# Extra identity products around the typed counts of a max pass over lanes, in a four-layer graph network

## The chip, the cores and the metric

The kernel runs on one core of one Trainium2 chip. Its time is the device time of one execution in microseconds; before the change it is 4076.91 us, the median of three runs (4075.01, 4076.91 and 4076.97 us).

## The reference

Four graph layers follow each other on 6,250 nodes of 128 values and 106,250 edges that are sorted by destination, with a residual and a layer normalisation after each. The change touches the third layer, whose core is a maximum over the edges of each node:

```python
msgs = z[edge_dst] @ Wd + z[edge_src] @ Ws + edge_weight[:, None] * ww[None, :] + bm
agg = jax.ops.segment_max(msgs, edge_dst, num_segments=n)
agg = jnp.where(deg[:, None] > 0, agg, 0)
hidden = jax.nn.relu(z @ W1[:H] + agg @ W1[H:] + b1)
x = layernorm(x + hidden @ W2 + b2)
```

The fourth layer sums messages whose weights depend on the type of an edge (0 or 1). For it the kernel builds matrices of counts, how many edges of a type go from a node to a node; these are the typed counts, and they are built during the max pass, for 27 of the 49 tiles of 128 nodes.

## The kernel before

**The max pass.** The edges are dealt out to 128 lanes (partitions), so that a lane holds a run of successive edges. Column `i` of all lanes is one step, and there are 831 steps, worked through in 208 chunks of four. A chunk passes through these engines:

- GpSimd (POOL) issues for each step one indirect DMA (L1834) that gathers the 128 source rows of the step, 512 bytes each, into `LANE_ROWS`, a ring of 32 steps. The instruction waits until the gather 16 steps back has landed, and at the first step of a chunk until TensorE is done with the chunk eight chunks back (semaphore `l2_turned`). GpSimd also gathers the maxima of finished nodes (L1822), and at the end of each of six segments a row per lane (L1806), for which it waits until the stored history of the last chunks of the segment has landed.
- TensorE (PE) puts the messages of a chunk into one of banks 0 to 2, in `messages`: a bf16 product for the edge weights (L1628, 512 columns) and one of the f32 identity with the gathered rows (L1631, 512 columns, which the trace shows as two matmuls), whose end raises `l2_turned`. It does this one chunk ahead of the rest.
- VectorE (DVE) takes the running maximum of the four steps out of the bank (L1711, four instructions that follow each other) into a history, which SyncE (SP) stores to memory. It raises `l2_scanned`.
- TensorE then makes one unit of typed counts, in `tensor_typed_counts`: eight bf16 products of one-hot matrices (L1153, 64 rows, 98 columns each), into banks 5 and 7. The last raises `typed_counted`. A unit waits until ScalarE has emptied the banks of the unit before (`typed_units`) and, for every other unit, for one-hot matrices that VectorE makes (L1168).
- ScalarE (ACT) empties the two banks with two casts (L1212) as soon as `typed_counted` is up, and raises `typed_units`.

So TensorE's order in the loop is: messages of chunk c+1, typed counts of chunk c, then the node work that a hand-made schedule (`max_schedule`) puts behind chunk c: transposes (L550), products with the f32 weights (L575, L1606, L1607). A chunk that ends a segment has a product more (`carry`, L1639), into columns 0 to 127 of bank 3 (`CARRY`), which ScalarE copies out (semaphore `rotations`). Columns 128 to 511 of bank 3 are not used in the pass.

The other layers multiply dense matrices of counts with rows split in three bf16 pieces; L2106 and L2125 are their products, of 384 columns in most layers, and L2171 their gathers on GpSimd.

Of the kernel before, what the change touches and what calls it, by code (L numbers as in the profile page):

```python
# [14 lines left out]
P = 128  # L15
# [28 lines left out]
CH = 4  # L44
# [83 lines left out]
SEGMENT = [0] + [-(-(-(-START[g] * N_ET // NT) + SEGMENT_MARGIN) // CH) * CH for g in SEGMENT_GROUPS[:-1]] + [N_ET]  # L128
SEGMENTS = len(SEGMENT_GROUPS)
# [4 lines left out]

FIRST_BANKS = ((0, 1), (2, 3))
CARRY = 3

# [78 lines left out]
def low(g):  # L218
    return banks_of(g)[:len(banks_of(g)) // 2]


def high(g):
    return banks_of(g)[len(banks_of(g)) // 2:]


def region(buf, g, width, half=0):
    words = GMAX * H2 // (2 if g >= NG - 2 else 1)
    at0 = (words if g == NG - 1 else 0) + half * words // 2
    return buf[:, at0:at0 + GROUPS[g] * width]


def blocks(buf, g, q, k=1):
    return [region(buf, g, k * P)[:, (k * q + b) * P:(k * q + b + 1) * P] for b in range(k)]
# [6 lines left out]
def parts(g, per):  # L240
    return [(b, q, min(per, GROUPS[g] - q)) for b, q in enumerate(range(0, GROUPS[g], per))]
# [135 lines left out]
def chunk_tiles(c):  # L377
    return range(c * CH, min((c + 1) * CH, N_ET))
# [166 lines left out]
def turn(k, g, src, width, banks, sem):  # L545

    n = 0
    for j in gtiles(g):
        for b in range(width // P):
            t = k.nc.tensor.transpose(k.bank[banks[n // 4]][:, n % 4 * P:(n % 4 + 1) * P],  # L550
                                      src(j)[:, b * P:(b + 1) * P], k.IDENT)
            n += 1
    t.then_inc(sem, 1)
# [16 lines left out]
def products(k, g, left, right, width, banks, sem):  # L570

    per = 512 // width
    for q in range(GROUPS[g]):
        for i, block in enumerate(left(q)):
            t = k.nc.tensor.matmul(k.bank[banks[q // per]][:, q % per * width:(q % per + 1) * width], block, right[i],  # L575
                                   start=i == 0, stop=i == len(right) - 1)
    t.then_inc(sem, 1)
# [546 lines left out]
def message_banks(g):  # L1124

    return (banks_of(g)[0], banks_of(g)[2]) if len(banks_of(g)) == 4 else banks_of(g)


def typed_unit(c):

    return divmod(c + UNITS, UNITS) if 0 <= c < UNITS * (len(TYPED) - 1) else None
# [6 lines left out]
def typed_banks(i, u):  # L1138
    return FIRST_BANKS[u % 2] if i == 0 else TYPED_BANKS


def tensor_typed_counts(k, i, u):

    T, unit, quarter = k.nc.tensor, UNITS * i + u, 4 * i + u // 2
    if u % 2 == 0:
        T.wait_ge(k.sem("typed_onehot"), quarter + 1)
    if i or u >= 2:
        T.wait_ge(k.sem("typed_units"), unit if i else unit - 1)
    for n in range(4):
        c = (4 * u + n) % QUARTER  # L1150
        for h in range(2):
            at = slice(REC * h, REC * h + REC)
            t = T.matmul(k.bank[typed_banks(i, u)[h]][:, n * KEYS:(n + 1) * KEYS], k.TSRC[quarter % 2][at, c, :],  # L1153
                         k.TKEY[quarter % 2][at, c, :], start=True, stop=True)
    t.then_inc(k.sem("typed_counted"), 1)
# [417 lines left out]
def parts_loaded(k, n):  # L1573
    return k.sem(f"load_parts_{n % 2}"), 16 * (n // 2 + 1)
# [20 lines left out]
def max_tensor(k, p):  # L1595
    T = k.nc.tensor

    def node(stage, g):
        if stage == "turn":
            T.wait_ge(*p.at("present", g))  # L1600
            turn(k, g, k.acc(H), H, low(g), p.sem(stage))
        elif stage == "first":
            T.wait_ge(*p.at("copy", g))
            for b, q, n in parts(g, 4):
                o = k.bank[high(g)[b]][:, 0:n * P]
                T.matmul(o, k.w1_2[:, 0, :], k.AUX3[:, START[g] + q:START[g] + q + n, :], start=True, stop=False)  # L1606
                t = T.matmul(o, k.w1_2[:, 1, :], region(k.ZT, g, P)[:, q * P:(q + n) * P], start=False, stop=True)  # L1607
            t.then_inc(p.sem(stage), 1)
        elif stage == "second":
            T.wait_ge(*p.at("relu", g))  # L1610
            products(k, g, lambda q: blocks(k.HT, g, q), [k.w2_2[:]], H, low(g), p.sem(stage))
        elif stage == "xturn":
            T.wait_ge(*p.at("normalise", g))
            turn(k, g, k.xt, H, high(g), p.sem(stage))
        elif stage == "parts":
            T.wait_ge(*p.at("xcopy", g))
            products(k, g, lambda q: [k.aux(START[g] + q)], [k.wdc[:, :, :].rearrange("p k h -> p (k h)")], H2,
                     message_banks(g), p.sem(stage))

    def messages(c):  # L1620

        tiles = chunk_tiles(c)
        n, slot, batch = len(tiles), tiles[0] % MAX_RING, c // PART_CHUNKS
        bank = k.bank[c % MAX_BANKS][:, 0:n * P]
        if c >= MAX_BANKS:
            T.wait_ge(k.sem("l2_scanned"), CH * (c - MAX_BANKS + 1))
        T.wait_ge(*parts_loaded(k, batch))
        T.matmul(bank, k.W9[:, batch % 2, c % PART_CHUNKS, :], k.WW9[:, 0:n * P], start=True, stop=False)  # L1628
        for i in tiles:
            T.wait_ge(*p.landed(i))  # L1630
        T.matmul(bank, k.IDENT, k.LANE_ROWS[:, slot:slot + n, :].rearrange("p t c -> p (t c)"), start=False,  # L1631
                 stop=True).then_inc(k.sem("l2_turned"), 1)

    def carry(s):

        T.wait_ge(k.sem("l2_scanned"), SEGMENT[s + 1])
        if s:
            T.wait_ge(k.sem("rotations"), 1 + s)
        T.matmul(k.bank[CARRY][:, 0:P], k.ROTATE, k.HIST[:, (SEGMENT[s + 1] - 1) % MAX_RING, :], start=True,  # L1639
                 stop=True).then_inc(k.sem("l2_carried"), 1)  # L1640

    T.wait_ge(k.sem("rotations"), 1)
    messages(0)
    for c in range(NCH):
        if c + 1 < NCH:
            messages(c + 1)
        if chunk_tiles(c)[-1] + 1 in SEGMENT:
            carry(SEGMENT.index(chunk_tiles(c)[-1] + 1) - 1)
        tensor_typed_counts(k, *typed_unit(c))
        for stage, g in p.due.get(c, ()):  # L1650
            node(stage, g)
    T.wait_ge(k.sem("typed_units"), UNITS * len(TYPED))
    for stage, g in p.tail:
        node(stage, g)
# [92 lines left out]
def max_scalar(k, p):  # L1747
# [29 lines left out]
    def carry(s):  # L1777

        A.wait_ge(k.sem("l2_carried"), s + 1)
        if s:  # L1780
            A.wait_ge(k.sem("l2_fixed"), s)
        A.copy(k.CARRIED, k.bank[CARRY][:, 0:P]).then_inc(k.sem("rotations"), 1)

# [1402 lines left out]
def dense_sync_l3(k, p):  # L3186
# [33 lines left out]
    "l1a": (dense_tensor_l1a, dense_vector_l1a, dense_scalar_l1a, dense_gpsimd_l1a, dense_sync_l1a),  # L3220
    "l1b": (dense_tensor_l1b, dense_vector_l1b, dense_scalar_l1b, dense_gpsimd_l1b, dense_sync_l1b),
    "l2": (max_tensor, max_vector, max_scalar, max_gpsimd, max_sync),
    "l3": (dense_tensor_l3, dense_vector_l3, dense_scalar_l3, dense_gpsimd_l3, dense_sync_l3),
}
# [694 lines left out]
```

## Time and profile before

| | |
|---|---|
| median of three runs | 4076.91 us |
| the profiled execution | 4070.89 us |
| its span, first to last instruction | 4066.8 us |
| TensorE, recorded busy | 2772.3 us, 68% |
| GpSimd, recorded busy | 2381.6 us, 59% |
| mean granted TensorE clock | 0.807 |
| the max pass in the span | about 1985 to 3400 us |

The profile is of one execution. "Idle before" is the time in which an engine did nothing recorded ahead of an instruction, and "<-" names what ended it: an instruction of another engine whose end lies just before, "issue" where no wait shows, and "remote" (in the chain "another core or an unknown queue") where the semaphore rose but no instruction that raises it had just ended. With one core there is no other core. The granted clock is a share of 2.4 GHz and has two levels, 1.00 (2.4 GHz) and 0.50 (1.2 GHz). Ends of matmuls are worked out by the profiler from their size; ends on the other engines are observed.

### The profile page before, as it was taken

The numbers are of one execution on the slowest core, as the hardware profiler recorded it, in microseconds if no ns is written. First come the engines' busy times: TensorE is split into PE (matmuls) and PEld (weight loads), VectorE is DVE, ScalarE is ACT, GpSimd is POOL, SyncE is SP. The second block draws the span as 40 slices with busy tenths as digits, with TensorE's granted clock in tenths as the row PEclk, the third lists the DMA queues.
The fourth block names the chain that finished last, engine by engine and source line by source line (L and its number), as shares of the span: only waits on it lengthen the run. The fifth ranks groups of instructions, "written<-read, shape, count | busy, mean of one in ns | idle before, by whom it ended". The sixth has DMA issues, their size and how long they took to land.

```text
span 4066.8 us, 48309 instructions
## 1 busy us (share of the span) xinstructions
PE 2772.3 (68%) x18224; PEld 1669.8 (41%) x18224; DVE 1410.9 (35%) x3599; ACT 854.8 (21%) x2326; POOL 2381.6 (59%) x2389
## 2 busy tenths in 40 slices
PE   3788787888798888888344443453453435989897
PEld 2444444555566777777111111121121112545454
DVE  6555564223231122212233332342343323233332
ACT  2555553222230111101111111221121112000000
POOL 3665662656626666664466656656555561777775
PEclk6899999889899999999555555665666556999998
DMA  5454444655546666664533432343343326656563
GB/s 149 152 175 153 162 168 157 194 179 187 189 154 206 202 196 195 201 201 141 145 125 125 143 124 86 124 133 116 111 129 125 113 93 222 227 198 230 198 224 128
DMA packets 299413, 658.89 MB, mean 162 GB/s; under 512 B 76555, under 2 KB 181976, under 8 KB 291624
## 3 DMA queue, kind: packets, MB, share of 16 engines
q1 hardware_dynamic: 188808, 404.50, 28.6%
q0 software_dynamic: 106784, 248.47, 21.3%
q8 instruction: 150, 2.46, 0.3%
q10 hardware_dynamic: 3584, 2.75, 0.2%
q14 instruction: 87, 0.71, 0.1%
HBM read 456.83 MB, written 198.69 MB: 161 GB/s over the span
## 4 chain that ended last, share of the span: by engine, by line
PE 47%; another core or an unknown queue 25%; issue 13%; ACT 8%; DVE 6%; DMA 1%; POOL 0%; ACTq 0%; SPq 0%; POOLq 0%; DVEq 0%
PE banks L2106 27%; PE banks L575 4%; PE banks L2127 4%; PE banks L2125 3%; PE banks L1631 3%; ACT arena L1212 3%; PE banks L550 1%; PE banks L2220 1%; ACT arena L2415 1%; PE banks L1153 1%; ACT x_nodes L612 1%; PE banks L1628 1%; ACT junk L624 1%; DVE arena L1711 1%
## 5 line engine op out<-in xcount | busy, mean ns | idle before, releaser
L2106 PE MATMUL banks<-arena 128*128 128x384 bf16 (+1 forms) x9310 | 1533.4, 313 | 119.5 <-issue 108.6
L2106 PEld LDWEIGHTS banks<-arena 128*128 128x128 bf16 x9310 | 906.6, 100 | 594.8 <-issue 203.4
L1834 POOL DMA_INDIRECT arena<-tab_l,ring_of_rows x831 | 798.7, 961 | 421.0 <-issue 281.1
L2171 POOL DMA_INDIRECT arena<-h_pieces,span_sources x450 | 434.6, 966 | 320.8 <-issue 111.4
L2171 POOL DMA_INDIRECT ring_of_rows<-message_pieces,span_sources x396 | 426.2, 1076 | 206.2 <-issue 100.1
L1153 PE MATMUL banks<-arena 64*128 64x98 bf16 x1728 | 98.5, 251 | 553.1 <-ACT arena L1212 349.5
L1711 DVE SCALAR_TENSOR_TENSOR arena<-arena,ring_of_rows,banks 128x128 f32<-128x128 f32 x830 | 288.2, 347 | 528.5 <-remote 233.3
L2171 POOL DMA_INDIRECT ring_of_rows<-x_pieces,span_sources x306 | 331.6, 1084 | 202.1 <-PE banks L2125 99.0
L2171 POOL DMA_INDIRECT ring_of_rows<-l_pieces,span_sources x306 | 298.1, 974 | 237.2 <-issue 70.9
L1212 ACT CAST arena<-banks 128x392 bf16<-128x392 f32 x432 | 188.3, 489 | 1157.3 <-remote 780.4
L1631 PE MATMUL banks<-arena,consts 128*128 128x512 f32 x416 | 361.0, 964 | 95.1 <-DMA arena<-tab_l,ring_of_rows 77.8
L2151 DVE TENSOR_TENSOR arena<-iota_bf,span_targets 128x768 bf16<-128x768 bf16 x243 | 134.9, 556 | 807.3 <-remote 343.7
L1153 PEld LDWEIGHTS banks<-arena 64*128 64x128 bf16 x1728 | 58.2, 114 | 810.1 <-issue 563.7
L2125 PE MATMUL banks<-ring_of_rows,arena 128*128 128x384 bf16 x1008 | 268.0, 335 | 16.9 <-issue 12.2
L2415 ACT CAST arena<-banks 128x392 bf16<-128x392 f32 x512 | 217.2, 493 | 197.9 <-PE banks L2220 117.0
L2127 PE MATMUL banks<-arena 128*128 128x256 bf16 x1350 | 182.1, 277 | 13.2 <-issue 12.9
L559 ACT COPY zt<-banks 128x512 f32<-128x512 f32 (+2 forms) x108 | 56.5, 549 | 588.9 <-remote 310.9
L1631 PEld LDWEIGHTS banks<-arena,consts 128*128 128x128 f32 x416 | 91.0, 272 | 179.1 <-issue 179.1
L550 PE MATMUL banks<-consts,arena 128*128 128x128 f32 x343 | 60.0, 311 | 130.5 <-DVE arena L659 50.4
L2127 PEld LDWEIGHTS banks<-arena 128*128 128x128 bf16 x1350 | 133.5, 99 | 36.3 <-issue 18.4
L1168 DVE TENSOR_TENSOR arena<-second_iota_bf,arena 128x784 bf16<-128x784 bf16 x108 | 60.7, 562 | 251.1 <-remote 228.9
L624 ACT ACTIVATE junk<-arena 128x256 bf16<-128x256 f32 (+1 forms) x196 | 73.9, 378 | 349.4 <-DVE arena L2859 138.7
(260 smaller groups left out, 2620.2 us busy)
## 6 DMA issues: line engine op xcount, KB each, us to landing
arena<-edge_counts SPq DMA_DIRECT2D x83, 896.0 KB
arena<-edge_counts SPq DMA_DIRECT2D x83, 672.0 KB
running_max<-arena SPq DMA_DIRECT2D x207, 256.0 KB
edge_counts<-arena SPq DMA_DIRECT2D x32, 1568.0 KB
typed_counts<-arena SPq DMA_DIRECT2D x27, 1568.0 KB
arena<-typed_counts SPq DMA_DIRECT2D x27, 896.0 KB
arena<-typed_counts SPq DMA_DIRECT2D x27, 672.0 KB
arena<-tab_l,ring_of_rows POOLq DMA_INDIRECT x831
```

Of the source, the lines that this page charges most:

```text
L575: t = k.nc.tensor.matmul(k.bank[banks[q // per]][:, q % per * width:(q % per + 1) * width], block, right[i], start=i == 0, stop=i == len(r ...
L1153: t = T.matmul(k.bank[typed_banks(i, u)[h]][:, n * KEYS:(n + 1) * KEYS], k.TSRC[quarter % 2][at, c, :], k.TKEY[quarter % 2][at, c, :], sta ...
L1212: t = A.copy(nodes[:, :, :, h, :], k.bank[typed_banks(i, u)[h]][:, 0:4 * KEYS].rearrange("p (i s r) -> p s i r", i=4, r=2))
L1631: T.matmul(bank, k.IDENT, k.LANE_ROWS[:, slot:slot + n, :].rearrange("p t c -> p (t c)"), start=False, stop=True).then_inc(k.sem("l2_turne ...
L1711: V.scalar_tensor_tensor(k.HIST[:, i % MAX_RING, :], before, k.SAME[:, i:i + 1], message, ALU.min, ALU.max).then_inc(k.sem("l2_scanned"), 1)
L1834: G.indirect_dma_start(k.LANE_ROWS[:, i % MAX_RING, :], None, k.tab["l2"], bass.IndirectOffsetOnAxis(ap=k.LANE_SRC[:, i:i + 1], axis=0)).t ...
L2106: t = T.matmul(k.bank[i % N_SUMS][:, 0:rows.shape[-1]], counts[:, s, :], rows, start=s == 0 and n == 0, stop=s == NT - 1 and n == len(term ...
L2125: return T.matmul(bank[:, 0:3 * H], weights, three, start=first, stop=last)
L2127: done = T.matmul(bank[:, 0:H2], weights, three[:, n * H2:(n + 1) * H2], start=first and n == 0, stop=last and n == 2)
L2151: V.tensor_tensor(k.OHG[p.layer][:, b % 2 * BATCH:(b % 2 + 1) * BATCH, :].rearrange("p c (v d) -> p c v d", d=2), k.IOTAB.rearrange("p (v ...
L2171: G.indirect_dma_start(k.rows[p.layer][s % n], None, k.pieces[p.layer], bass.IndirectOffsetOnAxis(ap=k.SRCG[:, at:at + 1], axis=0)).then_i ...
L2415: t = A.copy(nodes[:, :, :, h, :], k.bank[banks[h]][:, 0:4 * KEYS].rearrange("p (i s r) -> p s i r", i=4, r=2))
```

## The change

In the max pass TensorE gets two bf16 products ahead of the typed counts of a chunk and two behind them, each of the bf16 identity with the identity read three times: 128 rows, 128x128 weights, 384 columns. They write columns 128 to 511 of bank 3, which nothing reads, and raise no semaphore. Around the end of each segment two chunks are left out, so that the products keep clear of the copy of `carry`; with the constants of this kernel these are chunks 69, 70, 119, 120, 153, 154, 170, 171, 187, 188, 206 and 207, which leaves 196 chunks of 208. Ahead of the products of the chunks after a segment's end stands a wait for that copy.

```diff
+KEPT = 2
...
+    def keep_busy(n, c):
+
+        carried = [s for s in range(SEGMENTS) if c >= chunk_tiles(SEGMENT[s + 1] // CH - 1)[0] // CH]
+        if carried and c < SEGMENT[carried[-1] + 1] // CH + 1:
+            return
+        if carried:
+            T.wait_ge(k.sem("rotations"), 1 + len(carried))
+        for _ in range(n):
+            T.matmul(k.bank[CARRY][:, P:4 * P], k.IDB, k.IDB.unsqueeze(1).to_broadcast([P, 3, P]), start=True, stop=True)
+
...
         if chunk_tiles(c)[-1] + 1 in SEGMENT:
             carry(SEGMENT.index(chunk_tiles(c)[-1] + 1) - 1)
+        keep_busy(KEPT, c)
         tensor_typed_counts(k, *typed_unit(c))
+        keep_busy(KEPT, c)
         for stage, g in p.due.get(c, ()):
             node(stage, g)
```

## Rows read from the trace of the kernel before

**Rows 1.** The page: the span, and the granted clock in forty slices.

```profile
span 4066.8 us, 48309 instructions
...
PEclk6899999889899999999555555665666556999998
```

**Rows 2.** Busy time by stretch: the whole pass, then four short stretches.

```profile
core 0: us, PE busy (x) PEld busy (x) DVE busy (x) ACT busy (x) POOL busy (x), PEclk, DMA share, GB/s
1989.00:3390.00 1401.00, 615.57 (x2603) 222.66 (x2602) 492.54 (x1328) 240.25 (x549) 833.17 (x867) 0.60 0.37 119
2076.40:2081.40 5.00, 4.77 (x22) 1.75 (x22) 3.60 (x12) 1.84 (x5) 4.04 (x4) 0.50 0.31 93
2081.40:2085.20 3.80, 3.67 (x24) 1.09 (x22) 3.59 (x11) 0.87 (x2) 2.83 (x3) 1.00 0.50 153
2095.30:2104.60 9.30, 0.00 (x0) 0.00 (x0) 1.19 (x4) 0.00 (x0) 4.72 (x5) 0.50 0.25 71
2126.40:2137.90 11.50, 11.43 (x44) 3.34 (x40) 8.30 (x24) 2.62 (x6) 6.92 (x8) 0.50 0.35 115
```

**Rows 3.** Groups of instructions, forms kept apart, 1985 to 3400 us.

```profile
line engine op names shapes xcount | busy us, mean ns | idle before us <-releasers
L1834 POOL DMA_INDIRECT arena<-tab_l,ring_of_rows x816 | 784.2, 961 | 397.6 <-issue 257.7 <-remote 95.0 <-PE banks L1631 44.9
...
L1212 ACT CAST arena<-banks 128x392 bf16<-128x392 f32 x416 | 181.7, 489 | 1152.4 <-remote 780.4 <-issue 199.2 <-PE banks L1153 172.7
...
L1606 PE MATMUL banks<-arena 128*128 128x512 f32 x22 | 22.8, 1141 | 71.3 <-ACT zt L559 69.9 <-issue 1.5
```

**Rows 4.** Who waited for whom, 1985 to 3400 us.

```profile
engine line waited for: us in total, times, longest us
ACT arena L1212 <- remote: 780.4, 67, 41.7
...
PE banks L1153 <- ACT arena L1212: 348.0, 44, 24.4
...
POOL arena L1806 <- DMA running_max<-arena: 125.5, 6, 27.5
...
POOL running_max L1812 <- DVE arena L1720: 38.2, 5, 8.8
```

**Rows 5.** Timeline, chunks whose counts are taken at once, clock 0.50.

```profile
start us, us, engine line op out<-in xcount [idle before <-releaser]
2105.61 0.51 PE L1153 MATMUL banks<-arena 64*128 64x98 bf16 x8 [10.38 <-ACT arena L1212]
...
2106.16 0.87 ACT L1212 CAST arena<-banks 128x392 bf16<-128x392 f32 x2 [0.61 <-PE banks L1153]
...
2108.48 0.51 PE L1153 MATMUL banks<-arena 64*128 64x98 bf16 x8
...
2111.35 0.51 PE L1153 MATMUL banks<-arena 64*128 64x98 bf16 x8
```

**Rows 6.** Timeline, two chunks at clock 1.00.

```profile
2081.89 0.35 PE L1153 MATMUL banks<-arena 64*128 64x98 bf16 x8
...
2083.44 0.35 PE L1153 MATMUL banks<-arena 64*128 64x98 bf16 x8
```

**Rows 7.** Timeline, a chunk whose counts are taken late.

```profile
2092.32 0.51 PE L1153 MATMUL banks<-arena 64*128 64x98 bf16 x8 [7.25 <-ACT arena L1212]
...
2093.16 2.07 PE L1631 MATMUL banks<-arena,consts 128*128 128x512 f32 x2
...
2100.48 0.94 POOL L1834 DMA_INDIRECT arena<-tab_l,ring_of_rows  x1 [0.30 <-issue]
2104.68 0.87 ACT L1212 CAST arena<-banks 128x392 bf16<-128x392 f32 x2 [12.51 <-remote]
...
2105.45 0.94 POOL L1834 DMA_INDIRECT arena<-tab_l,ring_of_rows  x1 [4.02 <-remote]
```

**Rows 8.** Timeline, typed counts when GpSimd has just begun to gather.

```profile
1967.31 0.87 ACT L1212 CAST arena<-banks 128x392 bf16<-128x392 f32 x2 [0.50 <-PE banks L1153]
```

**Rows 9.** The chain in order of time, fourth layer: start, us, what.

```profile
3567.68 4.07 PE banks L2106 x12
...
3600.08 2.27 PE banks L2106 x14
```

**Rows 10.** Who waited for whom in the fourth layer, 3450 us to the end.

```profile
ACT zt L559 <- remote: 181.0, 8, 41.5
```

## The prediction

> **What bounds the kernel now.** I read the page first, then the busy time by stretch, the groups and waits of the max pass, the timeline and the chain. The page [rows 1] shows one long stretch, the max pass, in which TensorE's clock is granted at 0.5 to 0.6; everywhere else it is near full. By stretch [rows 2] the pass takes 1401 us, mean grant 0.60, and TensorE is recorded busy for 616 us of it, GpSimd for 833. Nobody is saturated, so the reader should look for a loop of waits.
>
> GpSimd's own floor: a gather is 0.94 us and 0.30 us to the next [rows 7], 1.25 us with rounding, so four steps are 5.0 us a chunk. 831 gathers, 49 of maxima and 12 at segment ends make 892 x 1.25 = 1115 us. The other 300 us or so of the pass is GpSimd waiting: 398 us idle before L1834 less 816 x 0.30 = 153 us [rows 3], and 125.5 + 38.2 us at the ends of segments [rows 4]. These are waits for the chunks to get through TensorE, VectorE and the history store.
>
> TensorE's side: at clock 0.50 free-running chunks follow each other every 2.87 us (counts start at 2105.61, 2108.48, 2111.35) and ScalarE takes the counts within 0.04 us of their recorded end [rows 5]. At clock 1.00 a chunk is 1.55 us [rows 6]. Either is faster than the 5.0 us of gathers, so TensorE ought to keep up. It does not because of what rows 7 show: the counts of 2092.32 have a recorded end at 2092.83, but ScalarE gets its semaphore at 2104.68, twelve us later, after GpSimd too had stopped and waited 4.02 us. TensorE recorded nothing in between (fourth stretch of [rows 2]). I call this a held release. Over the pass ScalarE lost 780 us in 67 such waits of 208 [rows 4], and TensorE's next unit waited behind ScalarE. Where GpSimd has only just begun to gather, the counts are taken at once [rows 8]. In the timeline the held releases lie inside long runs of gathers and end when such a run has stopped for want of ring space (3.2 us after it in rows 7); then some three chunks run freely, GpSimd restarts with the first of them, and a few us later the next release is held. The same happens in the fourth layer while TensorE streams products [rows 10], so a busy TensorE does not prevent it. I don't know its mechanism; that it belongs to the gathers is a reading.
>
> The Trainium skill (Perfetto Trace Analysis, Tensor Engine Instruction) says that the end shown for a matmul is computed, and that the semaphore goes up only when PSUM has acknowledged the write. Rows 7 agree that the two can part, here by 12 us; the page gives no cause, and the sum goes by ScalarE's observed start.
>
> **The change part by part.** It removes and moves nothing. It adds 196 x 4 = 784 products of 384 columns. Price: in the fourth layer 14 products of that size take 2.27 us, 0.162 us each, at clock 1.00; with the clock partly at 0.50 12 take 4.07 us, 0.34 each [rows 9]. I take 0.16 and 0.32, thus 0.65 or 1.3 us a chunk, 127 or 255 us of TensorE in all. Weight loads overlap, as in those rows.
>
> (a) Chunks whose release is held. The two products behind a unit and the two ahead of the next go out before TensorE blocks on `typed_units`, so they fall into the hold. With holds of 12 us on average (780/67) their 1.3 us is covered: nothing. If the cover were gone they would cost 67 x 1.3 = 87 us at most.
>
> (b) Chunks that run freely. 208 less 67 is 141; part of the 36 waits "for issue" (199 us [rows 3]) are holds whose semaphore record is missing, so I take 120. There TensorE is the bound of the burst: each product lengthens it, and late next are `l2_turned`, hence VectorE's maximum, the history store and GpSimd's ring, and `typed_counted`, hence ScalarE. A chunk is 4.17 us at 0.50 and 2.20 us at 1.00 against 2.87 and 1.55 now. Now the free chunks average about 2.6 us (2.87 mostly, 1.55 in the few full-clock stretches).
>
> (c) The clock. It decides (b). TensorE was recorded busy 4.77 of 5.00 us at 0.50 and then got 1.00; elsewhere 11.43 of 11.50 us, and stayed at 0.50 [rows 2]. So bursts stand at the edge of being granted full speed, and 384-column streams in the narrow-product part of a chunk should tip more of them. But a burst starts after an idle hold, so its beginning is at 0.50 whatever follows, 5 us of it in the one case where the grant rose (second stretch of [rows 2]). I take 1.2 chunks at 4.17 and 1.4 at 2.20: mean 3.1 us, 0.5 us more than now. 120 x 0.5 = 60 us.
>
> (d) What GpSimd absorbs. The timeline shows runs of 16 to 24 gathers, 4.6 chunks on average, with a 4 us wait behind each [rows 7]; they give now 5.0 + 4/4.6 = 5.9 us a chunk without the segment ends. If a slower burst costs a run 0.8 chunk, it is 5.0 + 4/3.8 = 6.05, and 208 x 0.18 = 37 us. Between 60 and 37 I take the middle, as I have no row that separates them: 48 us.
>
> (e) f32 node products in the second half (L1606 at 1141 ns [rows 3]) gain if the clock is up: at most a few tens of us; I take nothing, since they follow the same idle time. The wait for `rotations` stands two chunks behind the copy that ends it: nothing; upper bound, the 6 copies' 1 us each.
>
> Sum: profiled execution 4070.9 + 48 = 4119 us (span 4066.8 + 48 = 4115). The median lies 6 us above the profiled execution, so on it 4077 + 48 = 4125; I give 4122.
>
> **Bounds.** Everything free stays at 0.50: 120 x 1.3 = 156 us, 4233. All free chunks at full clock: 120 x (2.20 - 2.6) = -48 us, and with some 30 us from the node products -80, 4000.
>
> **Rivals.**
> 1. *Full clock carries the pass (faster).* The products keep TensorE granted at 1.00 from early in each burst: -48 to -80 us, 3997 to 4029. It decides once more than about four fifths of the free chunks run at full speed (4.17 - 1.97 x 0.8 = 2.6). For it: the edge seen in (c). Against: holds of 5 to 15 us with nothing to do, which four products of 1.3 us cannot fill. The Trainium skill (TensorE: Matmul & The Clock Gate, The HAM clock gate) holds that the half rate is the default and sustained activity lifts it; by that this rival is what the change would do, up to the idle gaps, which it says bring the half rate back. The drop to 0.50 by 2095.3 after an idle stretch [rows 2] agrees with the second part. Chance 0.24.
> 2. *Work behind the counts shortens the holds (faster).* In the fourth layer eight of ScalarE's waits are held [rows 10], but TensorE never stops there. If more matmuls behind a unit bring its semaphore up sooner, say 2 us in each of 67 holds, 134 us go, 3943; the floor is 1115 us plus the segment ends' 164. Against: the 12 us of rows 7 passed with a f32 product behind the counts already. Chance 0.10.
> 3. *The clock does not move (slower).* 4190 to 4233. For it: 11.43 of 11.50 us at 0.50. Chance 0.16.
> 4. *No change that shows.* The bursts' loss is all covered by GpSimd's 5.0 us a chunk, which also a chunk of 4.17 us does not exceed. For it: that very comparison. Against: GpSimd waits 300 us for TensorE's side. Chance 0.14.
> 5. My forecast, 4090 to 4170: chance 0.36.
>
> **How the numbers follow.** The measurement tells about 0.2%, 8 us. Slower 0.36 + 0.16 = 0.52, within 0.2% 0.14, faster 0.34. The range leaves out the extremes of rivals 2 and 3: 3990 to 4205. The likeliest case's own range is 4090 to 4170.
>
> **What the profile after would show.** Right: 784 new matmuls of 384 columns; free chunks at about 4.2 us at 0.50 and 2.2 at 1.00; mean grant in the pass up from 0.60 to some 0.65 to 0.75; about 60 to 75 waits of ScalarE "remote" with 700 to 800 us; GpSimd's waits in the pass up by some 50 us; nothing changed before 1985 us or in the fourth layer. Wrong, if the grant goes above 0.8 (rival 1), if ScalarE's remote waits fall by over 100 us (rival 2), or if GpSimd's idle time is what it was (rival 4).

## The result and the profile after

The changed kernel takes 4117.59 us, median of four runs (4102.11 to 4120.86), beside 4075.96 us for the kernel before in the same session (four runs, 4067.33 to 4076.97): a ratio of 1.0099 with a 95% interval of 1.007 to 1.0129, some 42 us slower. The profiled execution is the fastest of the four, 4102.11 us, so its trace shows only 31 us of the 42.

The page of the changed kernel, which answers to [rows 1]: span, granted clock in forty slices, and the groups of the new products (line, engine, operation, names, shapes, count, then busy us, mean ns and idle time before).

```profile
span 4098.2 us, 49877 instructions
...
PEclk6899998899999999999676766676676666999999
...
L1643 PE MATMUL banks<-identity_bf 128*128 128x384 bf16 x784 | 247.3, 406 | 0.0
...
L1643 PEld LDWEIGHTS banks<-identity_bf 128*128 128x128 bf16 x784 | 70.7, 112 | 184.2 <-issue 162.2
```

All 784 products are there. The slices of the pass went from 5 and 6 tenths to 6 and 7. Outside the pass the clock line is as it was, but for a tenth here and there.

Busy time by stretch of the changed kernel: the pass, all before it, all behind it (columns as in [rows 2]).

```profile
1989.00:3421.00 1432.00, 749.31 (x3357) 277.68 (x3357) 490.81 (x1327) 237.68 (x542) 846.56 (x875) 0.68 0.36 117
0.00:1985.00 1985.00, 1601.34 (x12385) 1118.27 (x12385) 702.47 (x1858) 569.41 (x1666) 1104.64 (x1108) 0.91 0.55 176
3421.00:4098.00 677.00, 568.57 (x3273) 330.37 (x3266) 216.58 (x415) 47.63 (x119) 434.41 (x403) 0.93 0.60 207
```

TensorE is recorded busy for 749 us in the pass, 134 more than in [rows 2], and its mean grant is 0.68 after 0.60. To place the 31 us I take three marks of each trace: the first typed counts of the pass, round which the first new products stand, the end of the last gather, and the end. Before, they lie at 1989.0, 3363.5 and 4066.8 us; after, at 2000.7, 3398.6 and 4098.2. So 12 us of the difference were there before the first added product, in code that is the same; 23 us lie in the pass, and 4 us came back behind it. A single pair of traces can't say more: the four runs of this kernel lie up to 19 us apart, and those of the kernel before up to 10, later up to 38. The same mark lies at 1995.1 to 2002.1 us in the traces of e1 to e4 below and at 2013.2 in that of h1, so what lies ahead of the pass scatters by as much as the pass itself grew here.

Who waited for whom in the changed kernel, 1985 to 3421 us, against [rows 4].

```profile
ACT arena L1213 <- remote: 841.9, 76, 49.0
...
PE banks L1154 <- ACT arena L1213: 386.6, 44, 36.8
...
POOL arena L1847 <- remote: 104.8, 32, 8.8
...
POOL arena L1847 <- PE banks L1632: 60.4, 29, 10.1
```

The held releases are still there, 76 for 842 us after 67 for 780. They did not go away. These waits are ScalarE's idle time, which also holds the time until TensorE has made the counts; how late ScalarE is behind the recorded end of the counts is the last column of the table below.

TensorE's timeline in the changed kernel: two chunks at half clock, a restart after a held release, two at full clock, and the next restart.

```profile
2089.43 0.51 PE L1154 MATMUL banks<-arena 64*128 64x98 bf16 x8 [8.98 <-ACT arena L1213]
2089.87 0.82 PE L1643 MATMUL banks<-identity_bf 128*128 128x384 bf16 x2
2090.62 0.61 PE L1629 MATMUL banks<-arena 36*128 36x512 bf16 x1
2091.16 2.07 PE L1632 MATMUL banks<-arena,consts 128*128 128x512 f32 x2
2093.03 0.85 PE L1643 MATMUL banks<-identity_bf 128*128 128x384 bf16 x2
2093.81 0.51 PE L1154 MATMUL banks<-arena 64*128 64x98 bf16 x8
...
2113.09 0.51 PE L1154 MATMUL banks<-arena 64*128 64x98 bf16 x8 [8.27 <-ACT arena L1213]
...
2117.05 0.35 PE L1154 MATMUL banks<-arena 64*128 64x98 bf16 x8
2117.34 0.50 PE L1643 MATMUL banks<-identity_bf 128*128 128x384 bf16 x2
...
2119.47 0.35 PE L1154 MATMUL banks<-arena 64*128 64x98 bf16 x8
...
2127.47 0.51 PE L1154 MATMUL banks<-arena 64*128 64x98 bf16 x8 [5.51 <-issue]
```

And the same stretch on ScalarE and GpSimd.

```profile
2112.07 0.87 ACT L1213 CAST arena<-banks 128x392 bf16<-128x392 f32 x2 [9.79 <-remote]
```

```profile
2108.74 0.94 POOL L1847 DMA_INDIRECT arena<-tab_l,ring_of_rows  x1 [0.30 <-issue]
2112.85 1.20 POOL L1847 DMA_INDIRECT arena<-tab_l,ring_of_rows  x1 [3.17 <-remote]
```

A free chunk now takes 4.38 us at the half clock (2089.43 to 2093.81), where [rows 5] had 2.87, and 2.42 us at the full one (2117.05 to 2119.47), where [rows 6] had 1.55. The pattern is that of [rows 7]: release held, gathers stop (the last one shown ends at 2109.68), release 2.4 us later, burst. The bursts begin at the half clock again (0.51 us for the counts at 2113.09 and 2127.47, after 8.3 and 5.5 us without work). In the second burst shown the counts run at full clock from its second chunk, in the first not yet. Over the whole pass, each of the 47 pauses of TensorE of over 5 us in this trace, and each of the 48 in the trace before, is followed by work at the half clock.

### The profile page after: what moved, and what is told of

It is laid out like the page before. It is cut to its first block, busy times and chain, and to the rows that moved or that the text cites. A ratio compares the mean times of both kernels' runs of the same rounds, so it can differ in the third digit from the quotient of the medians.

```text
span 4098.2 us, 49877 instructions
## 1 busy us (share of the span) xinstructions
PE 2919.2 (71%) x19008; PEld 1726.3 (42%) x19008; DVE 1409.9 (34%) x3599; ACT 854.7 (21%) x2326; POOL 2388.7 (58%) x2389
## 4 chain that ended last, share of the span: by engine, by line
PE 48%; another core or an unknown queue 23%; issue 12%; ACT 7%; DVE 6%; POOL 1%; DMA 1%; SPq 1%; ACTq 0%; POOLq 0%; DVEq 0%
PE banks L2119 27%; PE banks L576 4%; PE banks L2138 3%; PE banks L2140 3%; PE banks L1632 3%; ACT arena L1213 2%; PE banks L551 1%; PE banks L1643 1%; PE banks L2233 1%; POOL arena L1847 1%; ACT arena L2428 1%; PE banks L1154 1%; ACT junk L625 1%; PE banks L1629 1%
## 5 line engine op out<-in xcount | busy, mean ns | idle before, releaser
L2119 PE MATMUL banks<-arena 128*128 128x384 bf16 (+1 forms) x9310 | 1553.7, 315 | 129.9 <-issue 117.2
L1632 PE MATMUL banks<-arena,consts 128*128 128x512 f32 x416 | 309.6, 834 | 80.8 <-DMA arena<-tab_l,ring_of_rows 67.8
L1643 PE MATMUL banks<-identity_bf 128*128 128x384 bf16 x784 | 247.3, 406 | 0.0
L1643 PEld LDWEIGHTS banks<-identity_bf 128*128 128x128 bf16 x784 | 70.7, 112 | 184.2 <-issue 162.2
```

What stands on the lines that cost most here:

```text
L1643: T.matmul(k.bank[CARRY][:, P:4 * P], k.IDB, k.IDB.unsqueeze(1).to_broadcast([P, 3, P]), start=True, stop=True)
L2119: t = T.matmul(k.bank[i % N_SUMS][:, 0:rows.shape[-1]], counts[:, s, :], rows, start=s == 0 and n == 0, stop=s == NT - 1 and n == len(term ...
```

## The experiments

The kernels ran in four groups, each on one chip (e1 to e4, f1 to f4, g1 to g3, h1: four different ones) with runs of the kernel before beside them. Ratios are against those. For what lies inside the pass I count from the trace of each profiled execution: the pass runs from the first chunk that can have new products to the end of the last gather; a chunk is free when ScalarE begins on its counts less than 0.6 us after their recorded end, otherwise held; its pitch is the time to the next chunk's counts; "ScalarE late" is the sum over the held ones of how late it began. Each row on the pass is one execution, and the row "before" is the trace of the first session, whose chip is not on record. The traces are not all alike in how fast their execution was: e2's and h1's traces are of the slowest of their runs (4106.33 and 4188.93 us beside medians of 4087.08 and 4172.89), the changed kernel's is of its fastest (4102.11 beside 4117.59).

| kernel | before beside it, us | ratio (95%) | pass, us | grant in the pass | free chunks | their pitch: mean, median us | ScalarE late, us |
|---|---|---|---|---|---|---|---|
| before | | | 1374 | 0.60 | 119 | 3.79, 2.87 | 764 |
| changed | 4075.96 | 1.0099 (1.007 to 1.0129) | 1398 | 0.68 | 115 | 4.23, 3.88 | 735 |
| e1, four and four | 4078.74 | 1.0107 (1.0081 to 1.0133) | 1414 | 0.76 | 108 | 4.41, 3.07 | 723 |
| e2, ahead only | 4078.74 | 1.0014 (0.9993 to 1.0034) | 1398 | 0.66 | 113 | 3.94, 3.38 | 764 |
| e3, behind only | 4078.74 | 1.0025 (1.0001 to 1.005) | 1382 | 0.64 | 121 | 3.85, 3.64 | 714 |
| e4, 16 columns | 4078.74 | 1.0061 (1.0041 to 1.0081) | 1402 | 0.56 | 108 | 4.14, 3.17 | 742 |
| h1, eight and eight | 4080.55 | 1.0228 (1.0201 to 1.0255) | 1456 | 0.83 | 114 | 4.98, 4.37 | 626 |
| f1, GpSimd 16 ahead | 3447.20 | 1.0 (0.9987 to 1.0013) | 1111 | 0.59 | 207 | 5.40, 5.05 | 0 |
| f2, GpSimd 24 ahead | 3447.20 | 1.0 (0.999 to 1.0009) | 1110 | 0.58 | 207 | 5.40, 5.06 | 0 |
| g1, the change again | 3449.30 | 0.9989 (0.9978 to 1.0) | 1107 | 0.76 | 206 | 5.35, 4.93 | 1 |
| g2, as f1 | 3449.30 | 0.9995 (0.9986 to 1.0004) | 1111 | 0.58 | 207 | 5.39, 5.05 | 0 |
| f3, direct transfers | 3447.20 | 0.8742 (0.8726 to 0.8758) | 666 | 0.82 | 188 | 3.12, 2.48 | 29 |
| f4, f3 with the change | 3447.20 | 0.8824 (0.881 to 0.8839) | 687 | 0.91 | 205 | 3.40, 2.42 | 2 |
| g3, as f3 | 3449.30 | 0.8764 (0.875 to 0.8779) | 668 | 0.81 | 189 | 3.15, 2.49 | 26 |

### Place and number: e1, e2, e3

In e1 the number of products on either side is doubled; in e2 the call behind the counts is left out, in e3 the one ahead.

```
e1:  -KEPT = 2
     +KEPT = 4
e2:       tensor_typed_counts(k, *typed_unit(c))
     -    keep_busy(KEPT, c)
e3:  -    keep_busy(KEPT, c)
          tensor_typed_counts(k, *typed_unit(c))
```

> KEPT = 4: four products ahead of the typed counts and four behind, 1568 in all, twice the change. Column theory (each product costs its columns in the chunks that run freely, at the clock that is granted then): a free chunk is 5.5 us at 0.50 and 2.85 us at 1.00, against 4.2 and 2.2 with the change and 2.87 and 1.55 before; with half of them at full clock the mean is 4.2 us, 1.6 us over the 2.6 of before, but GpSimd's 5.0 us a chunk hides part: +90 to +150 us against before (4165 to 4225). Clock rival: with so many columns the full clock is kept through whole bursts, a free chunk is 2.85 us, and the loss is not larger than that of the change: +0 to +45 us, mean grant in the pass over 0.80.

> Two products ahead of the typed counts, none behind: half of the change. Column theory: half of its cost, +15 to +30 us against before, wherever the two stand. Place rival 1 (the products ahead delay the counts and with them ScalarE, the ones behind delay only the next messages, which VectorE takes later anyway): this half carries all of the loss, +35 to +45 us. Place rival 2 (the messages' end, which frees GpSimd, is what counts): both halves stand before the next messages, so again half of the loss.

> Two products behind the typed counts, none ahead. Column theory: +15 to +30 us against before, the same as the two ahead. Place rival 1: about 0. Rival that work behind the counts brings their semaphore up sooner: faster than before, ScalarE's remote waits under 700 us.

Either half costs 0.14% or 0.25% (8 and 7 us by the medians, where 15 to 30 were expected) with overlapping intervals, of which e2's includes no change. So no place is favoured. The half behind the counts did not make the kernel faster, and ScalarE's waits in its trace stayed above the 700 us under which they would have spoken for an earlier release (who waited for whom in e3, 1985 to 3400 us):

```profile
ACT arena L1213 <- remote: 751.7, 65, 38.6
```

The whole costs 0.99%, more than the two halves together (0.39%), but it was measured in another session and in four runs. Doubling it costs 1.07% (42 us), no more than the change itself within the intervals: in time the clock rival came true and not the 90 to 150 us of the column theory, though the grant stayed under the 0.80 that the rival asked for. The clock line of e1 shows the rise:

```profile
PEclk6899998899999999999687776786777777999999
```

The pass has 7 and 8 tenths now, 0.76 on average. With more full-clock chunks the median pitch of e1's free chunks is 3.07 us, under the 3.88 us of the changed kernel, though it has four products more; its mean is 4.41 against 4.23.

### The products without their columns: e4

The same 784 products with 16 columns in place of 384: the instructions and the weight loads stay, the streaming nearly goes.

```
-            T.matmul(k.bank[CARRY][:, P:4 * P], k.IDB, k.IDB.unsqueeze(1).to_broadcast([P, 3, P]), start=True, stop=True)
+            T.matmul(k.bank[CARRY][:, P:P + 16], k.IDB, k.IDB[:, 0:16], start=True, stop=True)
```

> The change with its 784 products cut from 384 columns to 16: same instructions, weight loads and wait, hardly any columns. Column theory: a free chunk is some 0.1 to 0.25 us longer (four weight loads of 0.1 us, in part overlapped), thus 0 to +15 us against before, and the mean grant in the pass stays at 0.60. Instruction rival (the number of instructions or weight loads, or the wait for the copy, is what costs): +30 to +45 us like the change.

It already costs 0.61%, some 26 us, where 0 to 15 were expected for next to no columns and 30 to 45 if the instructions were the whole cost: it lies between the two. Its timeline on TensorE at the half clock:

```profile
2106.20 0.51 PE L1154 MATMUL banks<-arena 64*128 64x98 bf16 x8 [3.81 <-ACT arena L1213]
2106.64 0.22 PE L1643 MATMUL banks<-identity_bf 128*128 128x16 bf16 x2
2106.80 0.60 PE L1629 MATMUL banks<-arena 36*128 36x512 bf16 x1
2107.33 2.07 PE L1632 MATMUL banks<-arena,consts 128*128 128x512 f32 x2
2109.20 0.25 PE L1643 MATMUL banks<-identity_bf 128*128 128x16 bf16 x2
2109.38 0.51 PE L1154 MATMUL banks<-arena 64*128 64x98 bf16 x8
...
2112.55 0.51 PE L1154 MATMUL banks<-arena 64*128 64x98 bf16 x8
```

A chunk takes 3.17 us against 2.87 in [rows 5]: 0.30 us for four products that stream next to nothing, 0.075 us each. The grant is 0.56, if anything below that of the kernel before. With all their columns four products cost another 1.21 us a chunk at the half clock (4.38 - 3.17), yet only another 0.4% in time. I put that down to the grant, which they bring from 0.56 to 0.68, while the fixed part of each product brings nothing back. The wait for the copy of `carry` is in both kernels, and no run takes it away by itself.

### Eight and eight: h1

```
-KEPT = 2
+KEPT = 8
```

> KEPT = 8: eight products ahead of the typed counts and eight behind, 3136 in all. A chunk of TensorE is 1.55 + 16 x 0.162 = 4.15 us at 1.00 and 8.0 us at 0.50. On a chip where the kernel before takes 3450 us GpSimd gives a chunk every 5.05 us: with full clock the chunk still fits and the kernel loses 0 to 15 us; if the clock stays at 0.50 for half of the time the mean is 6.1 us and it loses over 150 us. On a chip where the kernel before takes 4079 us: four and four cost 42 us, no more than two and two, since the clock rose from 0.68 to 0.76 in the pass; here the clock has no more than 0.1 to 0.2 to give and 8 more products add 1.3 us to a free chunk: +120 to +200 us. Clock rival, as for four and four: again no more than +45 us.

I had expected 120 to 200 us. It cost 92 (2.28%). Clock line, then TensorE's timeline of h1:

```profile
PEclk6899898899999999998798887897887777999998
```

```profile
2125.63 0.35 PE L1154 MATMUL banks<-arena 64*128 64x98 bf16 x8
2125.92 1.47 PE L1643 MATMUL banks<-identity_bf 128*128 128x384 bf16 x8
...
2128.60 1.46 PE L1643 MATMUL banks<-identity_bf 128*128 128x384 bf16 x8
2130.00 0.35 PE L1154 MATMUL banks<-arena 64*128 64x98 bf16 x8
```

Sixteen products at the full clock make the chunk 4.37 us, (4.37 - 1.55)/16 = 0.176 us each. With the grant at 0.83 in the pass the clock is nearly restored, and the kernel is slower still: a full-clock chunk with the filler is longer than a half-clock chunk without it (2.87 us). ScalarE begins 626 us late in all, 138 us less than before; I read that as filler which now runs inside the holds.

### Another chip: f1, f2, g1, g2

f1 and f2 were to shorten the runs of gathers, since a hold seemed to grow with their length: GpSimd may be only 16 or 24 steps ahead instead of 32.

```
-        if i >= MAX_RING and i % CH == 0:
-            G.wait_ge(k.sem("l2_turned"), (i - MAX_RING) // CH + 1)
+        if i >= LEAD_STEPS and i % CH == 0:
+            G.wait_ge(k.sem("l2_turned"), (i - LEAD_STEPS) // CH + 1)
```

> The kernel before, with one constant changed: at the first step of a chunk GpSimd waits for the chunk four chunks back (16 steps) instead of eight (32 steps). Nothing else differs, no products are added. Theory (a release is held while a run of gathers lasts, and ends some 3 us after GpSimd has stopped for want of ring space): runs get shorter, the mean held release falls from 8.7 us to 4 to 6, but GpSimd stops more often with 4 us each: about 5.0 + 4/3 = 6.3 us a chunk, +60 to +110 us (4140 to 4190). Rival (holds are periodic or come from TensorE's own state, whatever GpSimd does): mean hold stays near 8.7 us, and the pass loses more, since the ring covers less of each: over +150 us.

> As the run before it, with 24 steps instead of 32. Theory: between: mean hold 6 to 8 us, +15 to +50 us. Rival: as there, +50 us or more.

Neither moved the time, and neither could test the thought: on that chip the kernel before takes 3447.20 us (19 runs, 3442.71 to 3456.23), and in the traces of f1 and f2, which take as long, nothing is held. The changed kernel and f1 once more ran on another chip, where next to nothing is held either (one chunk of g1, by 0.8 us):

> The change itself once more, beside the kernel before on the same chip. The kernel before has taken 4079 us beside the runs e1 to e4 and 3447 us beside f1 to f4, and the trace of f1 shows not one held release. On a chip where the kernel before takes 4079 us: +1.0% as before. On one where it takes 3447 us GpSimd's gathers bound the pass (5.05 us a chunk, GpSimd waits 7 us in all): a chunk of TensorE is 4.2 us at 0.50 or 2.2 at 1.00 with the change, both under 5.05, so the change costs nothing, -7 to +10 us, up to +15 with the end of the pass. Rival (the loss is TensorE's columns wherever they stand): +0.5% or more, over +17 us.

> The kernel before with GpSimd's lead of 16 steps instead of 32, again. On a chip where the kernel before takes 3447 us: no change, as f1. On one where it takes 4079 us, the expectation of f1: mean held release down from 8.7 to 4 to 6 us and +60 to +110 us; if held releases do not depend on the length of the runs of gathers, over +150 us.

There the kernel before takes 3449.30 us (21 runs), and the changed one 3445.65: 0.11% less, with an interval that ends at no change. Busy time by stretch of f1 in its pass, and who waited for whom:

```profile
1709.00:2820.00 1111.00, 644.03 (x2569) 229.48 (x2565) 490.35 (x1320) 238.01 (x542) 843.40 (x868) 0.59 0.46 150
```

```profile
ACT arena L1213 <- PE banks L1154: 818.2, 189, 21.4
...
PE banks L1632 <- DMA arena<-tab_l,ring_of_rows: 432.7, 163, 8.7
```

The same two views of g1:

```profile
1704.00:2810.00 1106.00, 742.34 (x3344) 275.10 (x3343) 490.35 (x1319) 237.87 (x542) 834.62 (x866) 0.76 0.46 151
```

```profile
ACT arena L1213 <- PE banks L1154: 837.1, 192, 21.9
...
PE banks L1632 <- DMA arena<-tab_l,ring_of_rows: 339.3, 144, 8.2
```

ScalarE has no "remote" wait in these answers: it waits for TensorE's counts, TensorE waits for the gathered rows, and GpSimd issues one gather each 1.25 us almost without a break (its idle time over 0.30 us an instruction is 7 us in f1 and 12 in g1, against 282 in the kernel before). The pass is the 1115 us that the prediction gave as GpSimd's floor. In g1 TensorE is busy 98 us longer than in f1 and waits 93 us less for rows: the filler sits in that slack. The mean grant rose from 0.59 to 0.76 and bought nothing, since nobody waited for TensorE.

### Gathers taken out: f3, f4, g3

Here the 831 indirect gathers of the pass are direct transfers of fixed blocks of the same table. The maxima are then of other messages.

```
-        G.indirect_dma_start(k.LANE_ROWS[:, i % MAX_RING, :], None, k.tab["l2"],
-                             bass.IndirectOffsetOnAxis(ap=k.LANE_SRC[:, i:i + 1], axis=0)).then_inc(p.landed(i)[0], 16)
+        G.dma_start(k.LANE_ROWS[:, i % MAX_RING, :], k.tab["l2"][P * (i % NT):P * (i % NT + 1), :]).then_inc(p.landed(i)[0], 16)
```

> The kernel before with the 831 indirect gathers of the pass replaced by direct DMAs of the same size (128 rows of 512 bytes, of tile i mod 49 of the table) from the same GpSimd queue, into the same ring with the same semaphores and waits. The maxima and the layers after it are then of other messages. Theory (held releases belong to GpSimd's indirect gathers): they are gone but for those beside the node gathers, ScalarE's remote waits fall from 780 to under 100 us, chunks follow each other at 2.87 us at 0.50 or less, and the pass takes 600 to 900 us instead of 1401 (kernel 3300 to 3600). Rival (they come from TensorE's idle time or its clock): the waits stay at 700 us or so and the pass over 1200 us.

> The same direct DMAs in the kernel with the change. If the pass is then bound by TensorE's free chunks, the four products show their price in every chunk: 196 x 1.3 us = 255 us over the run before it if the clock stays at 0.50; 196 x (2.20 - 2.87) = -131 us, faster, if they bring full clock to a pass that was at 0.50 without them; 196 x 0.65 = 127 us if both are at full clock.

> The 831 gathers of the pass as direct DMAs from the same queue, again (the maxima and what follows are of other messages). On a chip where the kernel before takes 3447 us: 3015 us, as f3. On one where it takes 4079 us: if held releases belong to the indirect gathers, the pass shrinks to some 670 us, as in f3, and the kernel to 3350 +- 50 us; if they belong to GpSimd's queue whatever it issues, ScalarE keeps over 200 us of remote waits in the pass and the kernel stays over 3500 us.

They were meant to show whether the held releases belong to the gathers, and ran on the two chips that have none, so that question stays open. They answer another. Timeline of GpSimd in f3, then busy time in its pass (columns as in [rows 2]):

```profile
1999.93 2.64 POOL L1834 DMA_DIRECT2D arena<-tab_l  x5
2004.28 2.11 POOL L1834 DMA_DIRECT2D arena<-tab_l  x4 [1.71 <-PE banks L1631]
```

```profile
1706.00:2372.00 666.00, 470.79 (x2510) 182.27 (x2509) 469.02 (x1287) 232.19 (x528) 477.31 (x850) 0.82 0.74 246
```

Four steps take 2.11 us of issue instead of 5.0, GpSimd waits for TensorE in places, and the pass falls from about 1110 to 666 us. No engine fills it: GpSimd is busy 477 us, TensorE 471, VectorE 469. In this kernel the change costs 27 us (3042.26 - 3015.12), with full-speed chunks most of the time. That is none of the three outcomes that f4's expectation gave (255, -131 and 127 us): all of them priced the products in full in 196 chunks, and 27 us are 0.14 us a chunk. What takes up the rest was not followed. The same edit that cost nothing beside gathers costs again where GpSimd no longer sets the pace alone, and here ScalarE has no "remote" wait in either trace.

## Why the prediction was right

4122 us was forecast and 4117.59 measured, inside the likeliest case's own range. The direction, the size of the effect and the rise of the grant came out by the mechanism that was forecast; that the two times lie 4 us apart is in part luck. The forecast put all of its 48 us into the pass, while in the one trace there is the pass grew by 23, and 12 us came from ahead of it. By its steps:

**(a) Held chunks pay nothing: in line with the traces.** "ScalarE late" did not rise with the filler; it fell, 764, 735, 723 and 626 us for none, two, four and eight a side. That fits filler that goes into the hold, but 742 us in e4, whose products stream next to nothing, shows how little the first steps say; only h1's fall is large. ScalarE's own waits, 842 us in 76 after 780 in 67, lie just above the 700 to 800 us in 60 to 75 that the forecast named.

**(b) Free chunks pay: right in kind, mis-sized in its parts.** There were 119 (I took 120). Their mean pitch rose by 0.44 us where I had 0.5, their median by 1.01. Added up between the first and the last counts of the pass, the free chunks take about 453 us before and 488 after, 35 more and not 60, as there are four fewer of them; the held ones take 948 and 937. The same sums for other kernels don't all say that it is the free chunks that pay: against before, free and held chunks together take 24 and 22 us more in e1 and 117 more and 23 less in h1, but 6 less and 29 more in e2 and 6 less and 35 more in e4. Each is one execution, and how many chunks are held differs from one to the next (86 to 99), so the split is not settled.

The products are dearer than I priced them. I took the 0.162 and 0.32 us that a product costs in a long row of its like, and said that weight loads overlap. In the pass they stand in twos between other shapes, and a chunk came to 4.38 and 2.42 us where I had 4.17 and 2.20: (4.38 - 2.87)/4 = 0.38 us each at the half clock, and (2.42 - 1.55)/4 = 0.22 at the full one; e4 puts the part that has nothing to do with columns at 0.075 us, which is about the difference. In eights the price falls to 0.176 us. And the mean pitch before was 3.79 us, not the 2.6 from which I started: the ends of segments and other waits lie in it.

**(c) The clock: right in direction and size.** 0.68 lies in the range 0.65 to 0.75, and bursts start at the half clock as said. The Trainium skill (TensorE: Matmul & The Clock Gate, The HAM clock gate) holds that sustained activity lifts the clock; the grants of 0.60, 0.68, 0.76 and 0.83 for no, two, four and eight products a side agree. It paid part of the dearer products back, and e1 and h1 show how the repayment goes on (0.76, 0.83) without catching up.

**(d) What GpSimd absorbs: the least supported term.** I had set it to the middle of 60 and 37 us without a row for it, and no run measures it by itself. The pass grew by 23 us in the changed kernel and by 40 in e1 and 82 in h1. The expected 50 us more of GpSimd waiting came out as 19 (301 after 282), in the fastest execution of the four, and as 34 and 82 in e1 and h1 (316 and 364).

**(e) Node products and the wait for `rotations`:** no run takes either apart, and none shows in the time as forecast. The forecast that nothing changes ahead of the pass was missed by the 12 us above, in code that did not change.

**The rivals.** Rival 1 (full clock carries the pass) fell with h1: even at 0.83 the pass is longer. Rival 2 (work behind the counts shortens holds) fell with e3, +0.25%: its trace has 752 us of remote waits after 780, a fall far from the 134 us that the rival needed, and the changed kernel has 842. Rival 3 (the clock does not move) fell with the grant of 0.68; e4 is what it would look like in clock, though not in work. Rival 4 (GpSimd's 5.0 us a chunk cover it) was wrong on the chips of the forecast and is what happens on the two others. I gave it 0.14 against the 300 us that GpSimd waits; in the traces of f1, f2, g1 and g2, where next to nothing is held, it waits 7 to 12 us.

**What stays open.** The chips of the e kernels and of h1 hold releases in this program (before at 4078.74 and 4080.55 us) and two do not (3447.20 and 3449.30), with one program. The difference of some 620 us between the traces of before and f1 is spread: 280 us lie ahead of the pass, 264 in it, 76 behind it. What makes a chip do it was not found. That the holds come with gathers and end when they pause is seen in the timelines but no run took the gathers away on a chip that has holds, so it is argued, not shown. Nor is it known why all six traces of kernels with added products on chips with holds begin the pass 6 to 24 us later than the one trace before; on the chips without holds all seven begin it within 1704 to 1709 us. It is also not settled whether fewer steps ahead would shorten the holds, as f1 and f2 fell on a chip without them; nor why the whole costs more than the two halves together.

## What to carry to other kernels

Filler for TensorE's clock was worth its price in no kernel here. Where GpSimd sets the pace, it costs nothing and the higher grant buys nothing (0.59 to 0.76 for -0.11%); where TensorE works in bursts between pauses and others wait for it, the clock pays back only part of the filler. Whether it pays where TensorE works without pauses was not tried. Price a small product by a row with the same neighbours, not by a long row of its like. And run the kernel before on a second chip before a stretch of unexplained waits is made the basis of a change: here the pass waits for held releases on one chip and for GpSimd's issue on the next. The transfers of f3 (3015 us) bring other rows than the layer needs, so they are no replacement; they show how much of the time hangs on the gathers.

## What the runs showed of the hardware

- The same program takes 4079 and 4081 us on two chips and 3447 and 3449 us on two others (medians of 11 to 28 runs). Where it is slow, ScalarE takes counts up to some 40 us after the recorded end of TensorE's last product (38.6 us in the trace before, 44.3 after); in the traces of f1, f2 and g2 never more than 0.2.
- A bf16 product of 16 columns on 128 rows, two in a row between other shapes, adds 0.075 us at the half clock, far more than its columns (16/384 of 0.32 us are 0.013, an estimate from [rows 9]); one of 384 columns adds 0.38 us in twos; at the full clock 0.22 in twos, 0.176 in eights, 0.162 in [rows 9].
- TensorE's mean grant in the pass followed the filler, 0.56, 0.68, 0.76 and 0.83 for four 16-column products a chunk and for four, eight and sixteen of 384, but work behind a pause of over 5 us began at the half clock all the same, 47 times of 47 in the changed kernel and 22 of 22 in h1.
- GpSimd issues a direct transfer of a 128-row block in 0.53 us (2.11 for four), an indirect gather of as many rows in 1.25 us with the time to the next.
